# A deformable convolution's product of taps in two column halves of TensorE, and its offsets' product later

## The reference

```python
x = x + _L0_conv_ref(_gn(x), ...)   # 1x1 conv to 128 channels, a 3x3 depthwise conv with kernels made per image, mish, 1x1 conv back
x = x + _L1_conv_ref(_gn(x), ...)   # deformable conv
```

```python
val = gather(iy0, ix0) * (wy0 * wx0)[:, None] + gather(iy0, ix0 + 1) * (wy0 * wx1)[:, None] + gather(iy0 + 1, ix0) * (wy1 * wx0)[:, None] + gather(iy0 + 1, ix0 + 1) * (wy1 * wx1)[:, None]
val = val * mask[:, None]
return jnp.einsum('bikhw,oik->bohw', val, w_def.reshape(C2, c, KK))
...
cat = jnp.concatenate([xd, offset, mask], axis=1)
z = jnp.einsum('bihw,oi->bohw', cat, w_1x1[:, :, 0, 0]) + b_1x1[None, :, None, None]
z = z * inv[None, :, None, None] + (bn_beta - bn_mean * inv)[None, :, None, None]
return jax.nn.silu(z)
```

## Time and profile before

| | |
|---|---|
| time, median of 3 runs (lowest, highest) | 7632.61 us (7621.25, 7678.75) |
| profiled execution, from first to last instruction | 7541.7 us |
| PE busy, PEld busy | 4700.6 us (62%), 2152.1 us (29%) |
| DVE busy, ACT busy | 2782.6 us (37%), 2002.4 us (27%) |
| POOL busy | 5274.0 us (70%) |
| mean granted TensorE clock | 0.775 of full speed |
| moved by DMA | 698.39 MB, 93 GB/s |

### The profile page before, as it was taken

The page is one execution under the profiler, slowest core; times in us unless marked ns, Lnnn a source line. Parts: engine busy times, 40 slices in busy tenths (PEclk is TensorE's granted clock), DMA queues, the critical chain, the costliest instruction groups (busy, mean ns, idle before and its releaser), DMA issues.

```text
span 7541.7 us, 64796 instructions
## 1 busy us (share of the span) xinstructions
PE 4700.6 (62%) x16130; PEld 2152.1 (29%) x16130; DVE 2782.6 (37%) x3550; ACT 2002.4 (27%) x4101; POOL 5274.0 (70%) x4615
## 2 busy tenths in 40 slices
PE   6566566665766666665666665656567575665654
PEld 2232222222323222222323322322223232232322
DVE  4433424243342443424334242432424334243222
ACT  3222232322323222232222322223222232222211
POOL 1767767677776776767777776776767767677776
PEclk8777787777778778787777877778777787776776
DMA  3223333333323323333332333323323332332322
GB/s 83 86 87 101 89 90 92 95 98 89 103 88 90 101 88 102 90 90 99 90 104 87 93 97 89 99 89 90 96 85 101 92 100 88 93 91 88 97 89 83
DMA packets 307527, 698.39 MB, mean 93 GB/s; under 512 B 81553, under 2 KB 148881, under 8 KB 304849
## 3 DMA queue, kind: packets, MB, share of 16 engines
q0 software_dynamic: 221184, 604.27, 26.7%
q1 hardware_dynamic: 86043, 90.53, 5.1%
HBM read 639.23 MB, written 55.25 MB: 92 GB/s over the span
## 4 chain that ended last, share of the span: by engine, by line
PE 33%; another core or an unknown queue 30%; issue 21%; DVE 8%; ACT 6%; DVEq 1%; POOL 1%; ACTq 0%; DMA 0%; SPq 0%; POOLq 0%
PE tap_ps L464 10%; PE z_ps L469 9%; PE yo_ps L436 3%; DVE gat L891 3%; PE om_ps L436 2%; DVE yc L790 2%; PE tr_ps L397 2%; PE z_ps L455 2%; PE om_ps L397 1%; ACT val L642 1%; POOL gat L338 1%; PE xh_ps L387 1%; PE yo_ps L387 1%; ACT n_z L649 1%
## 5 line engine op out<-in xcount | busy, mean ns | idle before, releaser
L338 POOL DMA_INDIRECT gat<-patch_table,ixu x4608 | 5259.6, 1141 | 2251.7 <-issue 1520.9
L469 PE MATMUL z_ps<-val,w_tap 128*64 128x512 f32 x2304 | 1515.9, 748 | 1311.2 <-issue 864.8
L464 PE MATMUL tap_ps<-ident,gat 128*128 128x128 f32 x9216 | 1510.9, 317 | 707.0 <-DVE gat L891 533.1
L464 PEld LDWEIGHTS tap_ps<-ident,gat 128*128 128x128 f32 x9216 | 1229.1, 163 | 1653.3 <-issue 911.4
L642 ACT ACTIVATE val<-tap_ps 128x512 f32<-128x512 f32 x1152 | 685.1, 595 | 3733.1 <-remote 2072.5
L891 DVE TENSOR_TENSOR gat<-gat,wgt 128x1024 f32<-128x1024 f32 x1152 | 1369.0, 1219 | 430.8 <-DMA gat<-patch_table,ixu 352.3
L897 DVE SCALAR_TENSOR_TENSOR n_z<-n_z 64x512 f32<-64x512 f32 x128 | 87.9, 687 | 1861.3 <-ACT n_z L651 1235.0
L469 PEld LDWEIGHTS z_ps<-val,w_tap 128*64 128x64 f32 x2304 | 255.1, 155 | 1650.0 <-issue 1137.3
L455 PE MATMUL z_ps<-cat,w_cat 128*64 (+1 forms) x256 | 208.4, 910 | 367.7 <-ACT n_z L649 206.7
L790 DVE SCALAR_TENSOR_TENSOR yc<-xh,kb,yc 128x512 f32<-128x512 f32 x620 | 421.5, 746 | 1.9 <-issue 1.1
L436 PE MATMUL yo_ps<-np,w_om 128*41 128x512 f32 x768 | 378.0, 643 | 14.0 <-issue 13.7
(11 more groups left out here) (149 smaller groups left out, 3062.1 us busy)
## 6 DMA issues: line engine op xcount, KB each, us to landing
gat<-patch_table,ixu POOLq DMA_INDIRECT x4608
xb<-in_x SPq DMA_DIRECT2D x32, 1024.0 KB
patch_table<-rec SPq DMA_DIRECT2D x256, 128.0 KB
out<-oc SPq DMA_DIRECT2D x128, 128.0 KB
patch_table<-np SPq DMA_DIRECT2D x3, 1430.0 KB
kg_w<-in_kg_w SPq DMA_DIRECT2D x1, 576.0 KB, 6.8
patch_table<-rec_l SPq DMA_DIRECT2D x16, 32.0 KB
grid<-in_grid SPq DMA_DIRECT2D x1, 288.0 KB, 6.9
```

The costliest lines, as they stand in the source:

```text
L338: pool.indirect_dma_start(gat[:, k, t * 2 * REC:(t + 1) * 2 * REC], None, table_rows, bass.IndirectOffsetOnAxis(ixu[:, k, t:t + 1], 0)).th ...
L464: m = pe.matmul(tap_ps[k % 2][:, t * 128:(t + 1) * 128], gat[:, k, o:o + REC], ident[:, :], start=(d == 0), stop=(d == 1), is_transpose=True)
L469: pe.matmul(z_ps[0:C, :], w_tap[:, k - 1, :], val[:, (k - 1) % 3, :], start=False, stop=(k == KK)).then_inc(z_mm, 1)
```

## The change

Each product of a tap with its folded weights becomes two products of 256 columns. The first takes the first 256 pixels and writes partitions 0 to 63 of z_ps, and so stands on the lower 64 columns of the array; the second takes the other 256 pixels and writes partitions 64 to 127, on the upper 64 columns. Both use the same weights on all 128 rows, and both write columns 0 to 255 of the bank. The product of tap 0 now opens the sum. The offsets' product moves behind it, with the wait for the evacuation of the previous group in front of the product of tap 0. It is now two products of 256 columns too, over all 128 output columns, with a table of weights whose other half is zeros. ACT evacuates z_ps in two pieces of 64 x 256. What `zs_done` counts doubles.

```diff
--- before.py
+++ after.py
@@ -24,6 +24,7 @@
 CH = 512
+HALF = CH // 2
 NCH = PIX // CH
...
-        w_cat = sb("w_cat", [128, C])
+        w_cat = sb("w_cat", [128, 2, 2 * C])
...
+        def half(c, h):
+
+            return bass.ds(c * CH + h * HALF, HALF)
...
                 q = b * NCH + g
                 u0 = q * KK
-                if lo == 0:
-                    held(pe, "pe", zs_done, q + 1)
-                    held(pe, "pe", cat_done, (b + 1) * NCH)
-                    pe.matmul(z_ps[0:C, :], w_cat[:, :], cat[:, b % 2, span(g)], start=True, stop=False)
                 for k in range(lo, hi + (hi == KK)):
                     if k < KK:
                         pe.wait_ge(scaled, u0 + (k + 1))
...
                         m.then_inc(tap_mm, 1)
+                    if k == 1:
+                        held(pe, "pe", zs_done, q * 2 + 2)
+                        held(pe, "pe", cat_done, (b + 1) * NCH)
                     if k > 0:
                         pe.wait_ge(tap_done, u0 + (k + 2))
-                        pe.matmul(z_ps[0:C, :], w_tap[:, k - 1, :], val[:, (k - 1) % 3, :],
-                                  start=False, stop=(k == KK)).then_inc(z_mm, 1)
+                        for h in range(2):
+                            m = pe.matmul(z_ps[C * h:C * h + C, 0:HALF], w_tap[:, k - 1, :], val[:, (k - 1) % 3, HALF * h:HALF * h + HALF],
+                                          start=(k == 1), stop=(k == KK))
+                        m.then_inc(z_mm, 1)
+                    if k == 1:
+                        for h in range(2):
+                            pe.matmul(z_ps[:, 0:HALF], w_cat[:, h, :], cat[:, b % 2, half(g, h)], start=False, stop=False)
...
-            act.sem_inc(zs_done, 1)
+            act.sem_inc(zs_done, 2)
...
-                act.activation(zs[:, :], z_ps[0:C, :], ACT.Identity, bias=bn_shift[:, :], scale=bn_scale[:, :]).then_inc(zs_done, 1)
-                act.wait_ge(zs_done, q + 2)
+                for h in range(2):
+                    act.activation(zs[:, HALF * h:HALF * h + HALF], z_ps[C * h:C * h + C, 0:HALF], ACT.Identity,
+                                   bias=bn_shift[:, :], scale=bn_scale[:, :]).then_inc(zs_done, 1)
+                act.wait_ge(zs_done, q * 2 + 4)
                 act.activation(th[:, :], zs[:, :], ACT.Tanh, scale=0.5).then_inc(th_done, 1)
...
-    w_cat = np.zeros((128, C), np.float32)
-    w_cat[0:KK] = w_1x1[:, C:C + 2 * KK:2].T
...
+    w_cat = np.zeros((128, 2, 2 * C), np.float32)
+    for h in range(2):
+        w_cat[0:KK, h, C * h:C * h + C] = w_1x1[:, C:C + 2 * KK:2].T
...
```

More of the change, by code:

```diff
@@ L220, in build @@
             "kg_w1": kg_w1[:, :], "kg_w2": kg_w2[:, :, :], "w_om": w_om[:, :, :], "w_def": w_def[:, :, :],
-            "w_1x1a": w_1x1a[:, :], "w_cat": w_cat[:, :], "vec": vec[:, :], "b_1x1": b_1x1[:, :],
+            "w_1x1a": w_1x1a[:, :], "w_cat": w_cat[:, :, :], "vec": vec[:, :], "b_1x1": b_1x1[:, :],
             "kg_b2": kg_b2[:, :],
@@ L1033 @@
     arrays["w_1x1a"] = np.ascontiguousarray(w_1x1[:, 0:C].T)
-    w_cat = np.zeros((128, C), np.float32)
-    w_cat[0:KK] = w_1x1[:, C:C + 2 * KK:2].T
-    w_cat[KK:2 * KK] = w_1x1[:, C + 1:C + 2 * KK:2].T
-    w_cat[MROW:OM] = w_1x1[:, C + 2 * KK:].T
+    w_cat = np.zeros((128, 2, 2 * C), np.float32)
+    for h in range(2):
+        w_cat[0:KK, h, C * h:C * h + C] = w_1x1[:, C:C + 2 * KK:2].T
+        w_cat[KK:2 * KK, h, C * h:C * h + C] = w_1x1[:, C + 1:C + 2 * KK:2].T
+        w_cat[MROW:OM, h, C * h:C * h + C] = w_1x1[:, C + 2 * KK:].T
     arrays["w_cat"] = w_cat
```

## The result

The changed kernel takes 7680.44 us (median of 13 runs, 7637.59 to 7733.30), the kernel before 7625.03 us in the same measurement: ratio 1.0066, 95% interval [1.0038, 1.0094]. It is slower by 0.7%, where I had forecast 1.5% faster.

What follows compares the result with a forecast made beforehand. GpSimd, gathering or between gathers for 90% of the span, was taken as the bound. Halves 90 plus moved product 90, less 50 for late results and 17 for longer gathers, made 113 us: 7520 us from 7632.6, range 7390 to 7830.

Steps and rivals of the forecast that it cites:

- The bound: GpSimd works or is between gathers for 90% of the span; at most 730.8 us of index-copy waits can go.
- The halves on PE: Tap products on two column halves save 357 us of PE time, of which 90 us reach the end.
- three pass times: Split product on PE: upper 1 runs beside lower 2, so 0.64 us, 0.21 less at full clock.
- The rival that the halves run in turn: Rival (a), PE's products: halves don't overlap, only the moved product gains, 23 us, 7610 us; chance 0.26.
- I charge 50 us: Cost of PE's late results at a group's end, from 8 more instructions behind the copy: 50 us.
- as much again or nothing: Bounds of that charge: 8 more instructions could add another 6.5 us of lateness, or none.
- The moved product: Offsets' product behind tap 1's transposes shortens evacuation-to-gather from 6.69 to 3.25 us; 90 us at 39 first-tap stops.
- Gathers stretched by multiplies: GpSimd's gathers lengthen beside DVE's multiplies, 13% of working time; 130 us less waiting returns 17.
- Evacuation in two pieces: ACT's evacuation of z_ps takes 2 x 0.55 = 1.11 us, 0.34 more per group, at no cost to the end.
- Rival (b): More PE instructions make results reach ACT later, before tap copies and evacuations: 200 us slower, 7830 us; chance 0.32.

Runs made afterwards that it cites:

- the instruction count: Kernel before with each tap product as two of 256 columns, both on the lower half, evacuation whole: 7822.58 us on a late chip.
- instruction count and move: Kernel before with tap products split on one half (tap 0's whole) and the offsets' product moved; 1.005 is given for chips without late results.
- the move alone: Kernel before with only the offsets' product and the evacuation wait moved later, products and evacuation whole: 0.9918 on a late chip, 1.0054 on a quick one.
- the halves: Changed kernel with the offsets' product back at the group's head, column halves and two-piece evacuation kept: 7696.97 us on a late chip, 0.9985 on a quick one.

## Why the prediction was wrong, point by point

The measured 0.7% slower lies in the band within 1% of no change, to which I gave 0.24, and it is the small rest of large parts that nearly cancel.

- **The bound** was read rightly. The difference of the traces stands in GpSimd's waits for the index copies, and half of the gathers gone made the kernel 28% quicker.
- **The halves on PE**: I took three pass times, it is two. Of the value at the end I said 90 us, measured 125.6 us, on one late chip, against as many tap instructions without overlap. The rival that the halves run in turn is out. It rested on a rule of the Trainium skill (TensorE: Matmul & The Clock Gate, "Part 3: Packing small matmuls — row/col tiling") that a weight load overlaps a running matmul only when its row group differs; the rows above, with both halves on all 128 rows, contradict it, and the measurement decides. The same section counts about 4 ns of overhead for each tile. The trace agrees nearly: passes of the two halves start 6 to 7 ns apart.
- **"I charge 50 us" for late results is the step that failed.** Alone on a late chip the instruction count costs 167.5 us. In the comparison itself GpSimd's stops at first taps, which the moved product was to shorten by 90 us, grew from 202 to 360 us. I had the effect, its place (the last products of a group) and the price of one event, another 6.5 us; the trace of before shows 8.40 us before that evacuation, that of after 16.86. What I did was to choose a value near the lower end of "as much again or nothing". Had I taken as much again, at the 39 first-tap stops that I used for the gain, 39 x 6.5 = 254 us, the sum would have come out at 91 us slower. The rows gave no reason to prefer nothing, and one for the other end. The trace of before has 252 late releases before tap copies, 8.2 us each in the mean, so the lateness was common:

```profile
ACT val L642 <- remote: 2072.5, 252, 33.0
```

- **The moved product**: forecast 90 us, measured 56.6 us alone on a late chip, so right in sign and a third too large. From the evacuation's start to the gather are 5.10 us in the group end shown, not 3.25, since the copy of tap 0 comes late itself (1.78 us). I said that it costs nothing elsewhere. On quick chips it costs 0.5 to 0.6%, because it shifts DVE's work against the gathers; that I did not look for, though I had counted the gathers' stretching as a sum.
- **Gathers stretched by multiplies**: I said less waiting would give 17 us back. Waiting rose and gathers fell by 24 us; the exchange is the right one.
- **Evacuation in two pieces**: 1.11 us forecast, 1.15 measured.
- **Rival (b)** described what happened, though too dearly: it had the lateness before tap copies grow too (it fell, 2072.5 to 1745.6), and 200 us slower instead of 55. Its doubling of the 252.5 us before evacuations was an underestimate; it became 791.4. That the lateness would go from one place to the other was not in it.

**What stays open.** The parts measured alone on a late chip multiply to 1.0050 x 0.9918 = 0.997; the whole gave 1.0066 and 1.0028: the parts alone don't reproduce that the whole is slower. Even the upper ends of both, 1.0078 x 0.9950, make only 1.0028; the interval of the first measurement of the whole begins at 1.0038, that of the second at 1.0002. So the move may win less once the products are split, or late chips differ among themselves; the kernel that should have told it (instruction count and move) met quick chips only, and each part was measured on one late chip. What makes a release late, and why only on some chips, was not found. The runs show that splitting the products at equal columns brings late results before the evacuations, and that they nearly go when GpSimd has half the gathers, no more. Whether more instructions bring more lateness was tested at one dose only.

## What to carry to other kernels

Halving an operation onto two column halves of the array did run in half the time, but it doubles the instructions; whether that pays is decided by what is queued around it, not by the PE time saved. Take a step's effect on the phase between engines as an effect of its own: a moved instruction of 1 us on PE, with no wait on it, made gathers on GpSimd 40 us longer. And where a trace shows results that arrive late for no visible reason, price the term from the events it shows, keep both ends, and try the parts alone on more than one chip before believing either sign.

## What the runs showed of the hardware

- The same kernel takes 6510 to 6524 us on some chips and 7561 to 7655 us on others. On the late ones releases from PE arrive late while GpSimd gathers (some 2000 us of remote waits on ACT before tap copies, none on the quick chips), and GpSimd stops (684 to 731 us with the kernel before, none). The gathers are longer there too: of the 1027 us by which the move alone differs between the two (7584.0 and 6557.0), 708 are waits and 306 gathers. What the parts of the change are worth had opposite signs on the two.
- An indirect gather of 0.95 us that starts during a DVE multiply of two SBUF tensors lasts longer by what is left of the multiply, less some 0.12 us; one that starts before the multiply, with nothing else running on DVE, is not touched.
- Two products of 256 columns on the two column halves, each with all 128 rows, start 6 to 7 ns apart and take 0.58 us to the next transposes at full clock, where one of 512 takes 1.00 us.
- Shorter products lowered the mean granted clock each time: 0.775 to 0.738 with the change, 0.891 to 0.827 with half of the gathers. Twice as many instructions at equal columns left it at 0.827 to 0.829 on the quick chips, where the halves had 0.754 and 0.758.
